# Feature attention: two token tiles summed before its first scores, and full-array products among them

## The reference

```
x = x + _L2_ffn_ref(_layernorm(x, axis=-1), Wg, W1, W3, W2)        # 8 experts, top 2, hidden 704
x = x + _L3_xattn_ref(_layernorm(x, axis=-1), ctx_2048, ctx_2048)   # "feature attention"

def _L3_xattn_ref(q, k, v):            # q, k, v viewed as (groups, 8 tokens, 256 features)
    qk = jnp.einsum('bdm,bdn->bmn', qh, kh) * scale    # 256 x 256 scores between features
    sm = jax.nn.softmax(qk, axis=-1)
    ret = jnp.einsum('bmn,bcn->bcm', sm, vh)
```

## Time and profile before

| | us |
|---|---|
| median of three runs | 1143.98 |
| profiled execution | 1145.51 |
| its span | 1143.8 |
| mean granted clock of TensorE | 0.94 |
| PE busy | 1036.3 |
| DVE busy | 572.9 |
| ACT busy | 367.9 |
| POOL busy | 258.7 |

### The profile page before, as it was taken

How to read it: one execution, slowest core, us unless ns; L and a number is a source line. 1 busy time by engine, 2 the same in 40 slices (tenths; PEclk the granted TensorE clock), 3 DMA queues, 4 the chain that set the end, 5 groups by cost and what they waited for, 6 DMA issues and landing times.

```text
span 1143.8 us, 17531 instructions
## 1 busy us (share of the span) xinstructions
PE 1036.3 (91%) x6658; PEld 693.6 (61%) x6658; DVE 572.9 (50%) x1312; ACT 367.9 (32%) x687; POOL 258.7 (23%) x330
## 2 busy tenths in 40 slices
PE   5879999989999999979774999999849999998989
PEld 4666699457666767658653677777613443443467
DVE  6986423543434343455385112122166778556791
ACT  3652233232212121204210222122104666736660
POOL 4321431600000000003531222222132453202350
PEclk9995999999999999989985999999956999988999
DMA  9002032210101010065026112101060000020000
GB/s 285 27 2 101 19 97 84 88 38 29 38 14 38 24 38 5 11 229 226 1 99 223 28 33 102 37 28 42 19 227 1 2 1 1 2 73 1 0 10 28
DMA packets 37433, 67.26 MB, mean 59 GB/s; under 512 B 4456, under 2 KB 27080, under 8 KB 35816
## 3 DMA queue, kind: packets, MB, share of 16 engines
q1 hardware_dynamic: 29960, 51.98, 13.4%
q0 software_dynamic: 4080, 11.15, 3.4%
q10 hardware_dynamic: 3312, 3.02, 0.8%
HBM read 54.72 MB, written 11.40 MB: 58 GB/s over the span
## 4 chain that ended last, share of the span: by engine, by line
PE 76%; DVE 14%; ACT 3%; DMA 3%; issue 2%; POOL 2%; SPq 0%; DVEq 0%; ACTq 0%; POOLq 0%
PE bank L354 21%; PE bank L1255 12%; PE bank L1279 7%; PE bank L1605 6%; PE bank L2326 4%; PE bank L2351 3%; PE bank L2372 3%; PE bank L1615 3%; PE bank L2808 2%; PE bank L1268 2%; PE bank L1590 2%; PE bank L1580 2%; PE bank L2390 1%; PE bank L2814 1%; PE bank L1240 1%
## 5 line engine op out<-in xcount | busy, mean ns | idle before, releaser
L1255 PE MATMUL bank<-big 128*128 x552 | 147.7, 417 | 0.6 <-ACT big L1140 0.6
L354 PE MATMUL bank<-XNT,big 128*128 128x512 f32 x296 | 140.7, 626 | 5.4 <-DVE big L2554 2.8
L1255 PEld LDWEIGHTS bank<-big 128*128 128x128 f32 x552 | 98.1, 191 | 39.6 <-issue 2.7
L2326 PE MATMUL bank<-big,xs 32*128 32x512 f32 x256 | 88.5, 739 | 18.7 <-DVE xs L281 17.7
L270 POOL TENSOR_TENSOR rstd<-ve,half 128x1 f32<-128x1 f32 x48 | 27.5, 576 | 331.6 <-DVE ve L264 331.3
L354 PEld LDWEIGHTS bank<-XNT,big 128*128 128x128 f32 x296 | 56.6, 199 | 70.7 <-issue 62.0
L2181 DVE TENSOR_REDUCE big<-bank 128x2 f32<-128x512 f32 x128 | 81.9, 685 | 24.7 <-PE bank L2326 24.1
L1279 PE MATMUL bank<-big 128*128 (+1 forms) x368 | 87.2, 380 | 1.1 <-ACT big L1155 1.1
L1033 DVE TENSOR_TENSOR big<-big,bank 128x704 f32<-128x704 f32 x23 | 20.5, 889 | 124.9 <-ACT big L1148 124.9
L2272 ACT ACTIVATE big<-bank 128x1024 f32<-128x1024 f32 x64 | 64.9, 1024 | 38.9 <-PE bank L2351 38.6
L354 PE MATMUL bank<-CTXT,big 128*128 128x512 f32 (+1 forms) x192 | 67.0, 493 | 10.7 <-DMA big<-wvT 10.7
(11 more groups left out here) (351 smaller groups left out, 1807.2 us busy)
## 6 DMA issues: line engine op xcount, KB each, us to landing
big<-m_gu SPq DMA_DIRECT2D x8, 1408.0 KB
big<-m_d SPq DMA_DIRECT2D x8, 768.0 KB
big<-a_qk SPq DMA_DIRECT2D x16, 256.0 KB, 2.9
yg<-big ACTq DMA_DIRECT2D x23, 128.0 KB
big<-m_gu SPq DMA_DIRECT2D x8, 352.0 KB
big<-a_o SPq DMA_DIRECT2D x16, 128.0 KB, 2.1
xn<-XNT SPq DMA_DIRECT2D x8, 256.0 KB, 5.9
big<-f_keys SPq DMA_DIRECT2D x1, 2048.0 KB, 9.1
```

The costliest lines, as they stand in the source:

```text
L354: ins = e.matmul(out, a, b, start=start and n == 0, stop=stop and n == len(pairs) - 1)
L1255: ins = e.matmul(out, xgT[s % 2][:, kb, :], WB[:, bass.ds(at[s] + (kb * 2 * F + c * chunk), chunk)], start=kb == 0, stop=kb == KB - 1)
L2326: e.matmul(bank[:, step_bank(step), :], k.xs[t % 2][q, b * P:(b + 1) * P], cm[t % 2][q, 2 * jp:2 * jp + 2].rearrange("p j n -> p (j n)"), ...
```

## The change

Two tests ask whether `front` has an entry 6 instead of whether that entry is true. And TensorE gets products that nobody reads: identity times a part of the context, into bank 7. One of 128 columns stands behind each of the 16 scores of units 1 to 4, and four of 256 columns behind the front.

```
--- before.py
+++ after.py
@@ -1064,7 +1064,7 @@
             e.scalar_tensor_tensor(k.X[:, t], both[:, 1], wB[:, t:t + 1], k.X[:, t], ALU.mult, ALU.add)\
                 .then_inc(k.x_tile, 1)
 
-        if not shared_expert and k.front.get(6):
+        if not shared_expert and 6 in k.front:
             k.front[6]["combine"] = combine
             return
         for t in range(NT):
@@ -2214,7 +2214,7 @@
 
         def x_of(t):
 
-            if k.front.get(6):
+            if 6 in k.front:
                 k.front[6]["combine"](t)
                 e.wait_ge(k.x_tile, done0 - NT + t + 1)
 
@@ -2393,11 +2393,19 @@
 
         e.sem_inc(k.xt_ps, NT)
         after(e, "ld", 16)
+        def spare(n, w):
+
+            for _ in range(n):
+                e.matmul(bank[:, VB, 0:w], k.ident[:, :], k.CTXT[:, 0, 0:w], start=True, stop=True)
+
         for u in range(FRONT):
             for r in range(RG):
                 scores(u, r)
+                if u > 0:
+                    spare(1, P)
             if u == UNITS - 1:
                 turn_maxima(0)
+        spare(4, D)
         for u in range(NU):
             t = u // UNITS
             ahead = [(n, r) for n in units_ahead(u) for r in range(RG)]
```

## The result

The changed kernel takes 1165.94 us (median of 4, 1164.59 to 1167.6) where the one before takes 1143.53 (median of 4); ratio 1.0196, 95% interval 1.0173 to 1.0218. It is 22.4 us slower; 1167 was forecast, in 1151 to 1174. Its profiled execution took 1164.59, with a span of 1162.9.

What follows compares the result with a forecast made beforehand. DVE was taken to bound the front, TensorE the stage from 859.8 us. Front +23.8 (including -7.7), give-back -2.5 and sums +1.5 made +22.8: 1168.3 on the profiled execution, 1167 us as median, range 1151 to 1174.

Steps and rivals of the forecast that it cites:

- The test and the sums: Stage entrance: two tiles summed ahead of the first score instead of eight, so it starts 7.7 us sooner.
- sums 4 to 7: Tile sums moved into units 0 to 3, adding 1.0 us of DVE each; +1.5 us taken, bounds 0 and 4.0.
- sums 2 and 3: Tile sums after the front's last reduction, 2.0 us of DVE during the wide spares' 3.7 us: no cost.
- The last stage's weights: Six SP loads waiting for the last tile sum, moved from 841.8 to some 900 us: no cost.
- The spares part the scores: Front, units 1 to 4: spares between scores make the sixteen scores serial; 2.55 us a pair at half clock.
- "at most" of 2.63: Upper bound for one score and one spare at half clock: 2.07 + 0.69 - 0.13 us.
- the 40.8 forecast: Front: 16 pairs of one score and one spare at 2.55 us each, 40.8 us.
- Unit 0, the transposes with their wait, and the wide spares: Rest of the front: 2.0 us side by side, 1.0 after unit 3, and 3.7 for four spares at half clock.
- Half clock through the front: Main case, chance 0.80: serial scores never bring the clock back, so all the front runs at 0.50; 1160 to 1173.
- What was given back: Units 0 and 1 behind the wide spares: the clock rises soon, 15.6 us become 13.1, -2.5; bounds -5 and 0.
- POOL's sum: End of the front in the kernel before: the first L2351 came at 859.81 us, right after this POOL work.
- Rival 2: Front: full-array spares bring full clock, 1.43 us a pair, 1145 or 1140; turning point about 1.2 a pair; chance 0.11.

Runs made afterwards that it cites:

- e2: The change with all its spares, but all eight sums ahead of the feature stage as in the kernel before: 1172.7 us.
- e1: The change with its sums moved into the feature stage but without any spare product: 1135.7 us.
- e3: The change with its 16 narrow spares cut from 128 columns to 8, in the same places: 1164.2 us.
- e4: The change with its 16 narrow spares put four together behind the four scores of each of units 1 to 4: 1138.0 us.
- e5: The change plus 22 spares of 256 columns at the stage's entrance, where TensorE stood idle for 10 us: 1163.5 us.
- e9: The change without narrow spares, and with three spares of 256 columns, two behind unit 3's scores and one behind unit 4's: 1137.4 us.
- e12: The change without its 16 narrow spares, keeping only the four of 256 columns behind the front: 1139.6 us.

## Why the prediction was right

**The test and the sums.** From the last expert product to the first score 17.74 us became 10.15: -7.6 (forecast -7.7). The two tiles after unit 1 took 1.3 us more (forecast 1.5 for all of the units). I take that for sums 4 to 7; e2, whose sums stand ahead as before, has 0.4 of it too, so in the change they may have cost only 0.9. In e1 units 0 and 1, with sums 2 and 3 ahead of them and no wide spares above these, take 0.9 more (TensorE waits 0.75 for DVE at 858.78), which in the change is hidden as forecast. The last stage's weights were fetched from 906.6 on, and that stage was no longer for it (from the last L2372 to the end 143.3 us; 146.5 before).

**The spares part the scores.** Shown, by e3 and e4: hardly any columns in the same places leave the loss, all of them in other places remove it. The size was a little off: a pair 2.73 us at half clock, not 2.55, and over my "at most" of 2.63. I had taken the spare for two transposes (0.69), but it took 0.80: its second pass starts later after its first. The sixteen pairs took 43.3 us, the first and the last of them 2.6 each, so 2.5 more than the 40.8 forecast. Unit 0, the transposes with their wait, and the wide spares were 0.6 under together. Front 49.5 us, forecast 47.5.

**The clock.** Half clock through the front, as forecast from 862.6 to 870.2 of the kernel before. That row is less like the new front than I made it: its scores are let in one after another by DVE but overlap: eight start from 862.64 to 870.16, one every 1.1 us, where one alone takes 2.07. The conclusion carried over; the likeness was in part luck. e5 adds what the row could not show: serial work also loses a full clock. It gives a price too: at its 1.46 us a pair, sixteen pairs would take 23.4 us instead of 43.3 (an estimate), so some 20 of the 33.5 us lost in the front are the half clock, and with the scores parted the clock stays there. The Trainium skill (TensorE: Matmul & The Clock Gate, "Why this matters for your kernels") asks that TensorE be kept busy to get the full clock. For one score and one full product in turn this trace disagrees: TensorE was busy 42.14 of 42.20 us at a granted clock of 0.50.

**What was given back.** Units 0 and 1: 15.7 to 12.5, -3.1 (forecast -2.5), with the second fall of the clock that stood there as a bound.

**The sum.** -7.6 + 33.5 - 3.1 + 1.3 = +24.1 from the traces, forecast +22.8; the medians differ by 22.4. That the median came within 1.1 us of 1167 is closer than the terms were, so in part luck. The two profiled spans differ by 19.1 only, since the expert layer's last product happened to end 1.9 us sooner in the kernel after and its last stage was 3.2 shorter. That stage goes with its clock: the mean granted clock in it is 0.94 before (146.5 us), 0.98 after (143.3) and 0.99 in e1 (142.1), with no code of it changed. Over all the traces with an edit it is 142.1 to 145.2, and 143.8 in e2, whose entrance is that of before. I count neither to the change; why the clock there differs from run to run stays open.

**One reading was incomplete**, and did the forecast of the change no harm. I said that POOL's sum let the first L2351 start at 859.81. I overlooked the score ahead of it, which DVE's reduction lets start at 859.79. The two waits end within 0.03 us of each other, and the trace can't tell which of them would have held alone. But a spare between the two has to wait for the score in any case, so it isn't free, and that is where the expectations of e9 and e12 failed.

**One sum was wrong**, without weight. Rival 2 puts its turning point at a pair of 1.2 us; by its own terms (+1.3 us at 1.43 a pair, sixteen pairs) it is 1.35.

## What to carry to other kernels

Small products that run side by side on different rows of TensorE are one group: anything over all rows goes behind the group, never into it. A filler is free only where the next product would have waited anyway and doesn't share a start with the one ahead; ask this of each place, and what engine sets the pace there, since a full clock is worth little under another engine's pace. And test for a key with `in`: an empty dict as a flag cost this kernel 5.3 to 8.7 us.

## What the hardware showed that I had not expected

- A spare of 8 columns costs almost what one of 128 does between two scores at half clock: pairs of 2.53 and 2.73 us (e3 and the change). In a row, four spares of 128 columns take 2.08 us at half clock (e4, 840.01), 0.52 each.
- The full clock is lost, not only not regained, in work that keeps TensorE busy 5.16 of 5.20 us (e5).
- The clock rose behind 5.10 us of scores side by side with TensorE busy 5.04 (e1), and not in the 42.20 us of one score and one spare in turn with TensorE busy 42.14 (the change).
